# Attention scores in tiles of 32 feature rows, and a projection that adds onto a bias written by ScalarE

## The reference

```
x = x + 0.5 * ffn(layernorm(x))          # 256 -> 704 (silu gate * up) -> 256, inputs and weights rounded to FP4 in blocks of 16
x = x + attn(layernorm(x))
x = x + 0.5 * ffn(layernorm(x))

attn: q, k, v = split(x @ Wqkv.T + bqkv)                   # 16 heads of 16 features
      q = (elu(q) + 1 + 1e-4) / 4;  k = elu(k) + 1 + 1e-4
      num = q . cumsum(k v^T);  den = q . cumsum(k) + 1e-4   # causal, no softmax
      z = (num / den) @ Wout.T + bout
      out = layernorm(z) * gamma + beta
```

## Time and profile before

| | |
|---|---|
| time, median of 3 runs | 2227.42 us (2226.64 to 2227.62) |
| profiled execution | 2225.92 us, span of its instructions 2224.2 us |
| PE busy | 2124.0 us, 95% |
| DVE busy | 2066.5 us, 93% |
| ACT busy | 1915.0 us, 86% |
| POOL busy | 1897.5 us, 85% |

### The profile page before, as it was taken

The page is one execution under the profiler, slowest core; times in us unless marked ns, Lnnn a source line. Parts: engine busy times, 40 slices in busy tenths (PEclk is TensorE's granted clock), DMA queues, the critical chain, the costliest instruction groups (busy, mean ns, idle before and its releaser), DMA issues.

```text
span 2224.2 us, 91039 instructions
## 1 busy us (share of the span) xinstructions
PE 2124.0 (95%) x30384; PEld 1496.2 (67%) x30384; DVE 2066.5 (93%) x5231; ACT 1915.0 (86%) x4136; POOL 1897.5 (85%) x3002
## 2 busy tenths in 40 slices
PE   3899999999999899999999999979999999999998
PEld 1566666666666688888888888855666665666565
DVE  7999999999999689999999999978999999999997
ACT  7888888888888789999999999978888888888885
POOL 6899999999999678888888888868989999989996
PEclk9999999999999999999999999999999999999999
DMA  4765555555556432222222222224655555555555
GB/s 104 128 121 115 116 113 112 115 116 114 114 112 109 75 56 60 60 59 59 59 59 58 60 59 58 60 47 79 114 112 112 112 112 112 112 112 113 112 117 117
DMA packets 719856, 208.74 MB, mean 94 GB/s; under 512 B 666400, under 2 KB 719520, under 8 KB 719776
## 3 DMA queue, kind: packets, MB, share of 16 engines
q1 hardware_dynamic: 719776, 207.76, 46.5%
HBM read 20.38 MB, written 16.78 MB: 17 GB/s over the span
## 4 chain that ended last, share of the span: by engine, by line
DVE 41%; PE 25%; issue 13%; POOL 12%; DMA 4%; DVEq 2%; SPq 2%; ACT 1%; POOLq 0%; ACTq 0%
DVE ffn_y L748 10%; DVE ffn_per_block L717 9%; DVE ffn_hx L710 7%; PE ffn_ps_gu L860 6%; PE attn_ps_qk L1260 5%; DVE ffn_q L744 3%; PE ffn_ps_down L872 3%; DMA attn_xT<-attn_x_hl 3%; POOL ffn_h_hl L791 3%; POOL ffn_h_hl L790 3%; PE attn_ps_num L1300 3%; PE attn_ps_v_second L1276 2%; PE attn_ps_sc L1313 2%; DVE ffn_scale L723 2%; SPq L1033 2%
## 5 line engine op out<-in xcount | busy, mean ns | idle before, releaser
L860 PE MATMUL ffn_ps_gu<-wgu_hi,ffn_xT 128*128 128x512 f16 (+1 forms) x3072 | 739.0, 363 | 16.2 <-DVE ffn_hx L710 7.5
L860 PEld LDWEIGHTS ffn_ps_gu<-wgu_hi,ffn_xT 128*128 128x128 f16 x3072 | 300.9, 98 | 302.6 <-issue 21.7
L806 ACT ACTIVATE ffn_quarter<-ffn_y,offsets 128x960 int16<-128x960 f32 (+2 forms) x264 | 282.6, 1071 | 185.2 <-DVE ffn_y L748 185.2
L860 PE MATMUL ffn_ps_gu<-wgu_lo,ffn_xT 128*128 128x512 f16 (+1 forms) x1536 | 431.5, 363 | 0.0
L872 PE MATMUL ffn_ps_down<-wd_hi,ffn_hT 128*128 128x256 f16 x2816 | 349.9, 273 | 18.8 <-DVE x_sb L737 12.7
L790 POOL TENSOR_TENSOR ffn_h_hl<-ffn_q,ffn_h_scale_hi 128x704 f16<-128x704 f16 x256 | 352.2, 1376 | 12.5 <-DVE ffn_h_scale_lo L754 8.5
L791 POOL TENSOR_TENSOR ffn_h_hl<-ffn_q,ffn_h_scale_lo 128x704 f16<-128x704 f16 x256 | 354.0, 1383 | 0.0
L872 PEld LDWEIGHTS ffn_ps_down<-wd_hi,ffn_hT 128*128 128x128 f16 x2816 | 265.1, 98 | 99.0 <-issue 35.5
L717 DVE TENSOR_REDUCE ffn_per_block<-ffn_hx 128x60 f32<-128x960 f32 (+2 forms) x264 | 298.4, 1130 | 21.3
L748 DVE TENSOR_TENSOR ffn_y<-ffn_hx,ffn_per_block 128x960 f32<-128x960 f32 (+2 forms) x264 | 294.8, 1117 | 0.0
L842 ACT ACTIVATE ffn_odd<-ffn_quarter,offsets 128x960 f16<-128x960 int16 (+2 forms) x264 | 278.7, 1056 | 10.8 <-POOL ffn_shift L783 10.8
(11 more groups left out here) (184 smaller groups left out, 5177.6 us busy)
## 6 DMA issues: line engine op xcount, KB each, us to landing
x_sb<-in_L_attn_x SPq DMA_DIRECT2D x128, 128.0 KB, 2.4
out<-x_sb SPq DMA_DIRECT2D x128, 128.0 KB, 2.1
attn_v_eo<-attn_v_nat SPq DMA_DIRECT2D x256, 34.0 KB, 1.8
ffn_xT<-ffn_x_hl SPq DMA_TRANSPOSE x256, 2.4
ffn_hT<-ffn_h_hl SPq DMA_TRANSPOSE x256, 3.5
attn_xT<-attn_x_hl SPq DMA_TRANSPOSE x128, 2.4
attn_oT<-attn_o_hl SPq DMA_TRANSPOSE x128, 2.5
x_sb<-in_L_ffn_w_gate SPq DMA_DIRECT2D x2, 352.0 KB, 5.2
```

The lines of the kernel that those rows point to most:

```text
L806: nc.scalar.activation(quarter[:, back], y[:, back], ACT.Identity, bias=offsets[:, 0:1], scale=4.0 / HALF_MIN).then_inc(S["quarter"], 1)
L860: last = nc.tensor.matmul(ps_gu[par][:, a:b], xT[par][:, c, :], w[:, k, a:b], start=(n == 0), stop=(n == len(terms) - 1))
```

## The change

- Scores: a matmul now contracts over 32 feature rows (one pair of heads) with 64 columns. There are 32 of them a tile, on eight 32x64 tiles of the array. q needs no `q_rows` any more: `q_feat` serves. Each of the four pairs has its own PSUM bank; the numerators share two of these banks.
- The odd copy of k moves from POOL to ACT, in the place of the two `q_rows` instructions.
- TensorE makes the scores of tile i ahead of the numerators of tile i-1. DVE masks them at the end of step i, not at the head of step i+1.
- ACT writes the bias row (`rows[:, 0, :]`, scaled once) into the bank of z after `k_nat`, once `zg` of the tile before is read. The six products of z have start=False and add to it. The bias matmul, `ones3` and `bout3` are gone, and with them seven of DVE's small instructions in the first steps.
- Smaller: `of_pair` and its eps go, `odd_eps` comes; the second FFN stage waits at its first matmul for the last masked scores, and for the last o one tile later; the FFN's PSUM banks are laid out in another order.

```diff
@@ block.vector @@
-            for k in range(9):
+            for k in range(2):
                 of_attn.bias(dve, k)
                 ffn_step(dve, 3 + k, (3 + k) % 2)
+            in_order(dve, ffn_step, 5, FIRST)
@@ attention: PSUM @@
-        ps_sc = psum("ps_sc", [P, 2, DC, 2, 2, SUB])
-        ps_num = psum("ps_num", [P, 2, 512])
+        ps_sc_num = psum("ps_sc_num", [P, PAIRS, 512])
+        ps_sc = ps_sc_num[:, :, 0:DC * P].rearrange("p r (c s q) -> p r c s q", c=DC, s=2)
+        num = ps_sc_num[:, 2:4, DC * P:DC * P + WIDE].rearrange("p g (h w) -> p g h w", w=VW)
@@ vector_step: the mask moves from behind L1058 to the end of the step @@
+            if valid(i, N):
+                ready(dve, "scores_done", i)
+                if valid(tm, N):
+                    ready(dve, "num_done", tm)
+                nc.vector.tensor_tensor(scores[:]..., ps_sc..., causal[:]..., ALU.mult).then_inc(S["masked"], 1)
@@ gpsimd_step @@
-                nc.gpsimd.tensor_scalar(k_eo[par][:, :, :, 1, :], k, FEAT_EPS, odd[:], ALU.add, ALU.mult).then_inc(S["k_odd"], 1)
@@ scalar_step @@
-                for j in range(2):
-                    last = nc.scalar.activation(q_rows[par][:, :, j, :], expo[par][:, 0:DC, :], ACT.Identity, bias=of_pair_eps[:, j:j + 1], scale=of_pair[:, j:j + 1])
-                last.then_inc(S["q_rows"], 1)
+                nc.scalar.activation(k_eo[par][:, :, :, 1, :], expo[par][:, DC:2 * DC, :]..., ACT.Identity, bias=odd_eps[:], scale=odd[:]).then_inc(S["k_odd"], 1)
...
+            if valid(to, N):
+                if isinstance(to, int) and to == 0:
+                    act.wait_ge(F["added"], N)
+                freed(act, "z_gamma", to, 1)
+                nc.scalar.activation(ps_z[:, 0:D], rows[:, 0, :], ACT.Copy).then_inc(S["z_seed"], 1)
@@ tensor_step: scores, now ahead of the numerators @@
+                ready(pe, "k_even", i)
+                ready(pe, "k_odd", i)
+                ready(pe, "q_feat", i)
+                freed(pe, "masked", i, 1)
+                freed(pe, "o_ready", tn, 1)
+                for c in range(DC):
+                    for s in range(2):
+                        for a in range(2):
+                            for r in range(PAIRS):
+                                rows_of = slice(r * 2 * E, (r + 1) * 2 * E)
+                                last = nc.tensor.matmul(ps_sc[half(a), r, c, s], k_eo[par][rows_of, c, s, a], q_feat[par][rows_of, c, half(s)], start=True, stop=True)
-                                last = nc.tensor.matmul(ps_sc[half(a), g, c, s], k_eo[par][half(g), c, s, a], q_rows[par][half(g), c, :, half(s)], start=True, stop=True)
@@ tensor_step: z @@
-                freed(pe, "z_gamma", to, 1)
-                nc.tensor.matmul(ps_z[:, 0:D], ones3[:], bout3[:], start=True, stop=False)
+                ready(pe, "z_seed", to)
                 for n, (aT, w, k) in enumerate(terms):
-                    last = nc.tensor.matmul(ps_z..., aT, w[:, QT:, k], start=False, stop=(n == len(terms) - 1))
+                    last = nc.tensor.matmul(ps_z..., aT, w[:, QT:, k], start=False, stop=(n == len(terms) - 1), skip_group_check=True)
@@ ffn tensor_step, second stage @@
                 if half == 1 and isinstance(tg, int) and tg == 0:
                     pe.wait_ge(T["kv_first"], N)
+                    pe.wait_ge(T["masked"], N)
+                if half == 1 and isinstance(tg, int) and tg == 1:
                     pe.wait_ge(T["o_ready"], N)
```

More of the change, by code:

```diff
@@ L513, in tensor_gate_up @@
                 for j, a in enumerate(src):
-                    last = nc.tensor.transpose(ps[:, s % 3, j * P:(j + 1) * P], a, ident16[:])
+                    last = nc.tensor.transpose(ps[:, 1 + s % 3, j * P:(j + 1) * P], a, ident16[:])
                 last.then_inc(set_turned, 1)
@@ L915, in attention_constants @@
                      sb("rows", [P, 3, D]), sb("causal", [P, SUB]), sb("diag", [P, DC, 2 * PAIRS]), sb("even", [P, 1]), sb("odd", [P, 1]),
-                     sb("of_pair", [P, 2]), sb("of_pair_eps", [P, 2]), sb("eps2", [P, 2]), sb("own", [P, DC, PAIRS]), sb("ones3", [P, P], BF16), sb("bout3", [P, D], BF16),
-                     sb("feat_eps", [P, 1]), sb("keep", [P, N]))
+                     sb("odd_eps", [P, 1]), sb("eps2", [P, 2]), sb("own", [P, DC, PAIRS]), sb("feat_eps", [P, 1]), sb("keep", [P, N]))
 ATTN_PLACES = {"o": 8352, "oT": (1024, 2048), "o_hl": (9376, 4096), "mid": (5632, 6176), "before": (6720, 7264), "first": 7808, "second": 11264, "k_nat": 12352, "zg": 13376,
-               "k_eo": (15104, 17152), "scores": 19200, "v_nat": (23296, 24384), "v_eo": (25472, 27648), "q_feat": (29824, 30848), "q_rows": (31872, 33920),
+               "k_eo": (15104, 17152), "scores": 19200, "v_nat": (23296, 24384), "v_eo": (25472, 27648), "q_feat": (29824, 30848),
                "expo": (35968, 38016), "xT": (40064, 41088), "x_hl": (42112, 43136), "xn": 44160,
@@ L927, in attention @@
 def attention(nc, S, at, N, x_sb, A, ident, minus_half, eps, F, attn_added, set_up):
-    unscale, o_scale, one, rows, causal, diag, even, odd, of_pair, of_pair_eps, eps2, own, ones3, bout3, feat_eps, keep = (
-        A.unscale, A.o_scale, A.one, A.rows, A.causal, A.diag, A.even, A.odd, A.of_pair, A.of_pair_eps, A.eps2, A.own, A.ones3, A.bout3, A.feat_eps, A.keep)
+    unscale, o_scale, one, rows, causal, diag, even, odd, odd_eps, eps2, own, feat_eps, keep = (
+        A.unscale, A.o_scale, A.one, A.rows, A.causal, A.diag, A.even, A.odd, A.odd_eps, A.eps2, A.own, A.feat_eps, A.keep)
     with ExitStack() as scope:
@@ L1299, in tensor_step @@
                             h = c * PAIRS + r % 2 * 2
-                            nc.tensor.matmul(num[quarter(u), r // 2, h:h + 2, :], scores[:, r // 2, c, s, r % 2, quarter(m)], v_eo[oth][:, s, :, c * PAIRS + r, :],
+                            nc.tensor.matmul(num[quarter(u), r // 2, h:h + 2, :], scores[:, r, c, s, quarter(m)], v_eo[oth][:, s, :, c * PAIRS + r, :],
                                              start=(c == 0 and r % 2 == 0), stop=False, skip_group_check=True)
@@ L1365, in prepare_attention @@
     bias_in = sb([P, QT])
-    spare, rest = [sb([3, D]) for _ in range(2)]
-    part3 = [sb([3, D], BF16) for _ in range(2)]
     causal_all = sb([P, P])
-    in_pair = sb([P, PAIRS])
     step, top_ready, scaled, split = sem("qkv_step"), sem("qkv_top"), sem("qkv_scaled"), sem("qkv_split")
@@ L1466, in tops @@
         nc.vector.tensor_scalar(A.odd[:], A.even[:], -1.0, 1.0, ALU.mult, ALU.add).then_inc(done, 1)
-        dve.wait_ge(pair_ready, 1)
-        then(dve, nc.vector.tensor_tensor(of_pair[:], in_pair[:, 0:2], in_pair[:, 2:4], ALU.add))
-        nc.vector.tensor_scalar(A.of_pair_eps[:], of_pair[:], FEAT_EPS, None, ALU.mult).then_inc(done, 1)
+        nc.vector.tensor_scalar(A.odd_eps[:], A.even[:], -FEAT_EPS, FEAT_EPS, ALU.mult, ALU.add).then_inc(done, 1)
     def tops_made(pe):
```

82 lines of the change are left out of this document (24 added, 58 removed).

## The result

The changed kernel is slower: 2257.1 us in the median (2254.4 to 2258.6, 4 runs) against 2227.0 for the kernel before (2225.5 to 2227.6, 4 runs), a ratio of 1.0135 with a 95% interval of 1.0117 to 1.0152. The prediction was 2221.6, its range 2203 to 2240. The profiled execution took 2257.4 with a span of 2255.6, 31.4 above the span before. One execution among all that are reported here, one of `e11_waits_up` (2304.8 us), ran at a lower granted clock than its fellows and is left out of median and ratio.

What follows compares the result with a forecast made beforehand. It took a three-step loop through the transpose DMA (5.55 us a step) beside PE's 5.5 to 5.7 as the bound; -1 - 2.1 - 0.4 - 1.6 - 0.7 = -5.8 from 2225.9, median 1.5 higher: 2221.6 us, range 2203 to 2240.

Steps and rivals of the forecast that it cites:

- the way from qk to den: Attention loop's stretch from q and k matmuls to den, 3.65 us: moving the scores into it adds s + g.
- Rival 1: Longer way through TensorE costs more than POOL gives: loop 17.22 us, 5.74 a step, 2238 in all; chance 0.28.
- s + g: Time added to the loop by scores ahead of the numerators: 0.65 us, break-even at 0.79.
- s: New time of TensorE's score block: 0.55 us taken, between 0.43 and the numerators' pace of 0.82 to 0.91.
- g: TensorE's idle time at the extra switch of tile shape: 0.1 us taken, ends 0 and 0.24.
- My loop: Attention's chain den, `mv`, POOL, SP, transpose DMA of x, qk, numerators, den: 16.66 us over three steps, 5.55 a step.
- POOL -0.3: In the loop, one POOL instruction goes, so the low half of o starts 0.3 us earlier, then waits for ACT.
- DVE -0.2: In the loop, 0.3 us off the add into x, less 0.1 for the gap the mask filled.
- ACT: Two `q_rows` (1.08 us) go, odd k (0.49) and seed (0.40) come; seed fits ahead of `v_eo`, cost 0 to 0.3.
- The start, -2.5: Start of the program: -2.1 us from seven small DVE instructions gone, at most -0.4 from the removed `of_pair` instructions.
- The seams, -2.3: Stage ends: numerators wait less for DVE's mask, -1.6 us at the end of the stage, -0.7 at the first seam.
- The signs: Expected profile: den 4.2 us behind qk, DMA waits far above 0.14 a step, PE under 95%, step near 5.6.

Runs made afterwards that it cites:

- e11_waits_up: Changed kernel, with TensorE's waits and semaphore counts of the k-v products issued ahead of the 16 products with the states: 2272.2 us, ratio 1.0201.
- e14_xT_first_after: Changed kernel, with x's low half ahead of o's on POOL, xT ahead of oT on SP, z behind qk on PE: 2301.1 us, ratio 1.0339.
- e16_feat_up_after: e14_xT_first_after, with the features also ahead of den on DVE and mid ahead of `o_hl` on POOL: 2228.7 us, ratio 1.0016.
- e18_feat_up_only: Changed kernel, with only the features moved ahead of den on DVE: 2253.1 us, ratio 1.012.
- e3: Kernel before, with the scores ahead of the numerators, the mask at the step's end and z's bias from ACT: 2271.9 us, ratio 1.0207.
- e1: Kernel before, with only its 64-row scores ahead of the numerators and the mask at the end of DVE's step: 2270.4 us, ratio 1.0196.
- e2_seed: Kernel before, with only z's bias written by ACT and no bias matmul: 2230.7 us, ratio 1.0015.
- e12_split_ends: Kernel before, with each score matmul cut in two halves of 64 columns in the written-out steps only: 2238.3 us, ratio 1.0059.
- e6_split: Kernel before in its own order, with each score matmul cut in two halves of 64 columns: 2257.4 us, ratio 1.0141.

## Why the prediction was wrong

- *That the way from qk to den decides* was right: it was called what costs, and it did. Rival 1, the longer way through TensorE, is what came, and its condition, s + g over 0.79, was met; its price, 2238, was still 19 too low.
- *s + g, the step that failed first.* Taken as 0.65, measured 0.89, at the upper end for s (0.82 to 0.91) with nothing for g: PE's idle time at the switches from v to the numerators is 0.08 a step in the mean, before 0.09 (the 0.21 of the earlier trace rows was one step's). I chose near the lower end because the scores load 32 rows of weights; the row that was nearest, the 64 numerators at 13 ns, decided. With 0.89 my own sum gives 16.66 - 0.3 - 0.2 + 0.89 = 17.05, 5.68 a step, some 9 us dearer than forecast.
- *The ring I did not have.* My loop entered through `mv` and took three steps; the one that closes over o and SP's oT has 11.05 us in two steps before, 5.53, nearly as long as the one I added up, and it divides what is added by two, not three. In the changed kernel it has 11.48, 5.74 a step, and the step is 5.77. That it binds is shown by `e14_xT_first_after`, `e16_feat_up_after` and `e18_feat_up_only` together: cutting the ring of one step alone gains nothing, cutting that of two alone makes the other longer (6.18), and with both cut the step is 5.57. My loop through `mv` has room by then: POOL's shift is ready 0.30 ahead of ACT's xn in the mean, where 0.12 is the least seen. The SPq row is SP's issue of oT (L1033): the chain that I read ran through it, and I added it up as if it entered at `mv` alone.
- *POOL -0.3.* Nearly right: `o_hl` moved from 2.62 to 2.23 behind den in the mean and waits for ACT's half of o, as said.
- *DVE -0.2.* Half of it. The add into x fell from 0.78 in the mean (0.85 in the earlier trace rows) to 0.48, but `mv` comes only 0.09 earlier behind den.
- *ACT.* The odd k takes 0.59, not 0.49. The seed takes 0.39 (0.40 said); it waits for `zg` 0.28 in half the steps and costs nothing in this order (`e3` against `e1`).
- *The start, -2.5.* It was -4.1: with the seven DVE instructions gone PE is busy 20.00 of 20 us from 85 to 105, and `e2_seed` alone gives 2.8 of it. What gives the other 1.3 was not tried apart.
- *The seams, -2.3.* The step with the largest error, in sign too: with tiles 0 to 10, 115 to 127 and the tail +19.3. I priced only a wait for the mask, and no wait for the mask over 0.6 us is left there, as said, though PE now waits 1.28 at 1522.54 for ACT's seed. 13.9 are PE's stops, which I had no term for. `e12_split_ends` shows that more of PE's instructions make them, `e1_order` that the order makes some too, so the 13.9 can't be put down to one of the two. What is left is about what the slower clock behind them and the 0.15 a step of the rings come to, not measured apart.
- *The signs.* The waits of qk's loads grew from 0.14 to 0.38 a step and `o_hl` follows ACT's half, as said; den comes 4.55 behind qk where 4.2 was said, and PE is busy 96% where under 95% was said. The low end of the forecast's own range, 2211, is 2213 by its own sum.

Put together: start -4.1, loop +16.2 (tiles 10 to 115), ends and tail +19.3, sum +31.4, against -2.5, -1 and -2.3 forecast. The order and the size of s made the loop's part, PE's waits for its instructions most of the ends'.

## What to carry to other kernels

Where several engines are within 5% of the step, write down every ring with its length and its number of steps before moving a block ahead of an exit: what is added to a ring of two steps counts half in the step, to one of one step in full, and the cure for one (xT first) can cost 44 us in another. Price a block of small matmuls by the nearest measured pace of a whole block, 11 to 14 ns an instruction here, whatever its tiles could stream. And count the instructions in code that is passed only once: they are brought in while it runs.

## What the runs showed of the hardware

- 64 listed float32 matmuls of 32x64 on eight tiles take 0.89 us, 32 of twice the columns on four 64x64 tiles 0.87 to 1.03 (`before`, `e1_order`), 64 of half the columns on these four 1.13 (`e6_split`). The finer tiles gain little: 14 ns each, the numerators' 128x32 11 to 13 ns.
- Four waiting and counting instructions on PE's queue, moved ahead of the 16 products with the states, opened 0.19 us of idle array there (0.23 in the step shown) and took 0.13 off the time behind them (`e11_waits_up`).
- Stops of 0.7 to 2.5 us inside blocks of small matmuls, only where code is passed for the first time; each ends 1.2 to 1.7 us behind the end of an instruction packet of 16 KiB.
- ScalarE writes a PSUM bank and matmuls with start=False add onto it, here in the bank of z, which matmuls write tile after tile; the write of 256 columns takes 0.39 us. No run here shows it for a bank that no matmul has written.
